# A two-layer graph kernel on one core: lookups moved from the node stage into the next stage, and logits alternated between two PSUM banks while the attention stage fills

## The reference, cut to what matters

```python
# x: 50000 nodes x 128; src, dst: 12500 edges, sorted by dst; edge_attr: 12500 x 128
def sage_mean(h, Ws, Wn, b):                      # twice, with relu between
    agg = segment_sum(h[src], dst); deg = segment_sum(1, dst)
    return h @ Ws + agg / max(deg, 1) @ Wn + b
x = layernorm(x + sage_mean(relu(sage_mean(x))))
# attention with 4 heads over the same edges, on the new x
q, k, v, e = x@Wq+bq, x@Wk+bk, x@Wv+bv, edge_attr@We+be
alpha = einsum('ehd,ehd->eh', q[dst], k[src] + e) / sqrt(128)
attn  = softmax of alpha over the edges of one dst
out   = segment_sum((v[src] + e) * attn, dst) + x@Wskip + bskip
x = layernorm(x + elu(layernorm(out)*ln_g + ln_b) @ Wlin + blin + x))
```

## Time and profile before

| what | value |
|---|---|
| time, median of 3 runs (lowest, highest) | 1630.11 us (1629.76, 1630.32) |
| the profiled execution: its own time, its span | 1631.72 us, 1629.9 us |
| PE busy | 1502.5 us, 92% |
| DVE busy | 1291.4 us, 79% |
| ACT busy | 1177.9 us, 72% |
| POOL busy | 1029.4 us, 63% |
| mean granted TensorE clock | 0.979 |

### The profile page before, as it was taken

How to read it: one execution, slowest core, us unless ns; L and a number is a source line. 1 busy time by engine, 2 the same in 40 slices (tenths; PEclk the granted TensorE clock), 3 DMA queues, 4 the chain that set the end, 5 groups by cost and what they waited for, 6 DMA issues and landing times. The chain is left out here.

```text
span 1629.9 us, 33886 instructions
## 1 busy us (share of the span) xinstructions
PE 1502.5 (92%) x7879; PEld 1046.4 (64%) x7879; DVE 1291.4 (79%) x6158; ACT 1177.9 (72%) x3174; POOL 1029.4 (63%) x1038
## 2 busy tenths in 40 slices
PE   4999999999999998899789977999999999999985
PEld 3777777777777776788556643555555555555543
DVE  5999999999999999566568864777777777777773
ACT  2999999999999998344257751677777777777773
POOL 2888888868888885577177627456555555556421
PEclk9999999999999999899989998999999999999997
DMA  2567666654444443233169863233333333333220
GB/s 79 143 162 154 158 155 163 153 152 149 149 147 149 149 148 125 61 96 95 58 195 291 283 213 93 79 85 89 88 90 86 86 89 89 89 83 89 72 51 8
DMA packets 156183, 199.52 MB, mean 122 GB/s; under 512 B 36159, under 2 KB 79342, under 8 KB 156070
## 3 DMA queue, kind: packets, MB, share of 16 engines
q1 hardware_dynamic: 127450, 160.43, 32.6%
q0 software_dynamic: 27200, 36.26, 10.2%
q10 hardware_dynamic: 1420, 1.60, 0.3%
HBM read 106.66 MB, written 100.07 MB: 127 GB/s over the span
## 5 line engine op out<-in xcount | busy, mean ns | idle before, releaser
L1379 POOL DMA_INDIRECT big<-x_tab,look x196 | 199.1, 1016 | 92.9 <-issue 36.8
L1396 POOL DMA_INDIRECT out_dram<-big,idx x98 | 99.5, 1015 | 222.6 <-PE pb L1448 146.4
L737 PEld LDWEIGHTS pb<-MG_s,big 128*128 128x128 f32 x832 | 149.5, 189 | 128.6 <-ACT big L770 112.5
L737 PE MATMUL pb<-MG_s,big 128*128 128x256 f32 x832 | 207.4, 392 | 26.6 <-ACT big L770 26.5
L746 ACT ACTIVATE big<-big 128x128 f32<-128x128 f32 x416 | 180.2, 482 | 0.0
L1668 DVE CUSTOM_DVE_ANT_0 big<-pb,big,zero 128x128 f32<-128x128 f32 x392 | 120.3, 348 | 72.7 <-PE pb L1491 72.5
L719 PE MATMUL pb<-C_s,big 128*128 128x128 f32 x832 | 161.6, 276 | 0.0
L720 PE MATMUL pb<-Ws1c_s,big 128*128 128x128 f32 x832 | 161.4, 276 | 0.0
L868 POOL TENSOR_TENSOR big<-big,cl 128x512 f32<-128x512 f32 x104 | 133.6, 1284 | 36.8 <-DVE big L842 35.8
L1108 POOL DMA_INDIRECT big<-h1e_tab,hidx x98 | 97.9, 999 | 73.0 <-POOLq L1916 33.0
L1508 PEld LDWEIGHTS pb<-Wg_s,big 128*128 128x128 f32 x784 | 103.8, 194 | 49.9 <-issue 41.9
(11 more groups left out here) (356 smaller groups left out, 4017.1 us busy)
## 6 DMA issues: line engine op xcount, KB each, us to landing
big<-in_x_dram SPq DMA_DIRECT2D x104, 256.0 KB
x_tab<-big SPq DMA_DIRECT2D x98, 256.0 KB
out_dram<-big SPq DMA_DIRECT2D x98, 256.0 KB, 2.1
c_ve<-ve_tab SPq DMA_DIRECT2D x98, 256.0 KB, 2.8
ve_tab<-c_ve SPq DMA_DIRECT2D x66, 256.0 KB
h1e_tab<-a_rows SPq DMA_DIRECT2D x25, 256.0 KB, 2.6
x_tab<-a_rows SPq DMA_DIRECT2D x25, 256.0 KB
big<-in_edge_attr_dram SPq DMA_DIRECT2D x97, 64.0 KB
```

Source lines behind the costliest of these rows:

```text
L737: t = pe.matmul(o, b_x1T[:, r * P:(r + 1) * P], MG_s[:], start=True, stop=True)
L1379: g.indirect_dma_start(out=o, out_offset=None, in_=x1_tab, in_offset=bass.IndirectOffsetOnAxis(ap=look[:, a, j:j + 1], axis=0), bounds_che ...
```

## The change

It has two parts.

**Lookups.** The slots for the small transfers in a node-stage turn are numbered anew: a turn with a source gather now has one of them, all others two. The redirect writes end in turn 53 instead of 49, the lookups begin in turn 55 (`LOOK_AT` = 101) and go on through turn 103, the last; by then 91 of the 98 are issued. The other seven, the wait for all of them and the four operations that make `hidx` move to the end of `a_pool`, in the first sampling stage. The helpers between `b_pool` and `a_pool` only change their place in the file.

**Logits.** In the fill, tiles 1, 3, 5, 7 and 9 have their logits in `VB` instead of `PB`. PE then waits for the logits of two tiles ago instead of one. Since `VB` first holds the tables of turn 0, the product of tile 1 waits for DVE's copy of them (`g_fol`), and the first values product, in turn 10, waits for the logits of tile 9. For tiles in `VB`, DVE's unused full-size output goes to `d_vex` instead of `d_junk`.

```diff
+        LOOK_AT = NT + 3
+        B_LOOKS = 2 * TILES - 4 * R - LOOK_AT
+        assert 0 < B_LOOKS < NT and TILES >= 6 * 4 * R
+        def look_up(g, e):
+            g.indirect_dma_start(out=look[:, 0, e:e + 1], out_offset=None, in_=redirect,
+                                 in_offset=bass.IndirectOffsetOnAxis(ap=idx[:, SRC, e:e + 1], axis=0),
+                                 bounds_check=N - 1, oob_is_err=False).then_inc(dma_k[e % 4], 16)
...
-                if it % 6 == 5 and it < 96:
+                brings = it % 6 == 5 and it < 6 * 4 * R
+                if brings:
                     gather_src(g, it // 6 // R, it // 6 % R)
-                for t in range(2 * it, 2 * it + 2):
+                slot = 2 * it - min(it // 6, 4 * R)
+                for t in range(slot, slot + (1 if brings else 2)):
...
-                    elif t >= TILES and t - TILES < NT:
-                        if t == TILES:
+                    elif t >= LOOK_AT:
+                        if t == LOOK_AT:
                             for k in range(4):
                                 g.wait_ge(dma_p[k], 16 * len(range(k, NT + 1, 4)))
+                        look_up(g, t - LOOK_AT)
             g.wait_ge(s_row, 16 * (TILES // 8 + (1 if spread < E else 0)))
...
+        def a_pool(g):
+            for s in range(4, NG):
+                after(g, "a_pmT", s - 4)
+                for r in range(min(R, NT - R * s)):
+                    gather_src(g, s, r)
+            for e in range(B_LOOKS, NT):
+                look_up(g, e)
             for k in range(4):
                 g.wait_ge(dma_k[k], 16 * len(range(k, NT, 4)))
             g.tensor_scalar(hf[:, 0, 0:NT], look[:, 0, 0:NT], float(N), float(FAR), ALU.is_lt,
...
+        def logit_bank(a):
+            return VB if a < LAG and a % 2 else PB
...
                     if b == 0:
                         pe.wait_ge(step("g_fol"), RUNS)
+                        after(pe, "d_al", LAG - 1)
                     values(b)
...
                     after(pe, "d_xT", a)
-                    after(pe, "d_al", a - 1)
-                    pe.matmul(PB[:], X(a, 0), Aqk_s[:], start=True, stop=False)
+                    after(pe, "d_al", a - 1 if a > LAG else a - 2)
+                    if a == 1:
+                        after(pe, "g_fol", 0)
+                    pe.matmul(logit_bank(a)[:], X(a, 0), Aqk_s[:], start=True, stop=False)
...
-                    pe.matmul(PB[:], X(a, 2), Aqe_s[:], start=False, stop=True).then_inc(step("d_pP"), 1)
+                    pe.matmul(logit_bank(a)[:], X(a, 2), Aqe_s[:], start=False, stop=True).then_inc(step("d_pP"), 1)
...
-            return v.tensor_tensor_reduce(hs(d_junk, h), hs(PB, h), d_x1d[a % XD], SCALE, zero[:, 0:1],
+            junk = d_vex if logit_bank(a) is VB else d_junk
+            return v.tensor_tensor_reduce(hs(junk, h), hs(logit_bank(a), h), d_x1d[a % XD], SCALE, zero[:, 0:1],
```

More of the change, by code:

```diff
@@ L995, in a_pool @@
                     gather_src(g, s, r)
+            for e in range(B_LOOKS, NT):
+                look_up(g, e)
+            for k in range(4):
+                g.wait_ge(dma_k[k], 16 * len(range(k, NT, 4)))
+            g.tensor_scalar(hf[:, 0, 0:NT], look[:, 0, 0:NT], float(N), float(FAR), ALU.is_lt,
+                            ALU.mult).then_inc(s_look, 1)
+            g.tensor_scalar(hf[:, 1, 0:NT], look[:, 0, 0:NT], float(-N), None, ALU.add).then_inc(s_look, 1)
+            g.wait_ge(s_look, 2)
+            g.tensor_tensor(hf[:, 1, 0:NT], hf[:, 0, 0:NT], hf[:, 1, 0:NT], ALU.add).then_inc(s_look, 1)
+            g.wait_ge(s_look, 3)
+            g.tensor_copy(hidx[:, 0:NT], hf[:, 1, 0:NT]).then_inc(s_look, 1)
+            g.wait_ge(s_look, 4)
         def a_dve(v):
```

## The result

The changed kernel took **1618.63 us** (median of four runs, 1617.88 to 1619.28) against 1630.00 for the kernel before (1629.76 to 1630.32): 11.4 us less, ratio 0.993, 95% interval 0.9913 to 0.9947. The forecast was 1627.4 with a range of 1626.1 to 1629.0, and most of its chance on a difference too small to measure. The gain came out at four times the 2.7 us of the forecast.

The account below looks back on a forecast made before the run. The prediction took DVE to bound the node stage, POOL's DRAIN its end, and PE the attention stage after a serial fill. Fill 2.3 + node-stage end 0.4 = 2.7 us off 1630.11: 1627.4, range 1626.1 to 1629.0.

Parts of the forecast that it names:

- the first term of the change: Node stage: spreading the lookups takes one small transfer out of 16 turns, changes no DVE, PE or ACT instruction; worth 0.
- DVE waiting for L878: Node stage: a sign in the changed kernel's profile that would show the prediction wrong; no size given.
- POOL's last lookup: Node stage's end: lasting 1.40 instead of 1.00 beside DVE's L837, it would end at 648.9, leaving nothing of 0.4.
- POOL's list sets nothing there as long as its addition L868 is in time: Node stage: DVE busy 595.4 of 609 us, POOL 489; L868 waits for DVE, not DVE for it.
- The node stage's end: Stage ends with POOL's DRAIN; lookups end at 648.5, DRAIN 7.4 later: gain 0.4 us, between gain 1.0 and loss 0.2.
- The operations moved: First sampling stage: seven lookups, their landing and four operations end with POOL's DRAIN at about 800, SP 809.0; cost 0.
- The fill: Attention's fill: with two logits banks PE no longer stands before each product; gain 2.3 us, bounds 0.9 and 3.2.
- Turn 1: Fill: tile 1's product waits for DVE's copy of turn 0's tables, starting at 989.09 instead of 988.17; loss 0.9.
- Tile 1's wait: Fill: PE's wait before tile 1's product, expected at about 1.8 us.
- the values': Fill: PE's wait before the first values product, for tile 9's logits, expected at 1 us or more.
- slower: the clock: Fill: PE's longer wait before tile 1's product drops its clock to the lower level; about 1636 us; chance 0.05.

## Why the prediction was wrong, step by step

- **The step that failed** is the first term of the change: "Spreading them changes no instruction of DVE, PE or ACT. It takes one small transfer out of each of the 16 turns with a source gather; with DVE nearly full in any case that is worth 0." The first sentence is true of the list and false of the durations. The term measured 9.9 to 10.1 us. DVE's 595.4 busy of 609 was read as work, but 10 of them were DVE held in one instruction. The question that was not asked: is each duration of DVE's the same in all turns? One query for L817 would have given 147, 154 and 1247 ns as its least, median and longest. The sign of error that the prediction named for this stage, DVE waiting for L878, couldn't show it: the hold leaves no wait in the trace.
- **The contention was weighed in one direction, and by half of its rule.** The prediction had the earlier trace rows: POOL is held when DVE has the way to SBUF. It costed this for POOL's last lookup alone. The trace of before shows the reverse 16 times, DVE held while POOL's addition has it. The Trainium skill (SBUF — State Buffer, SBUF: two separate sides) states it both ways: whichever of a DVE instruction "in a 2-port perf mode, or with two SBUF inputs" and a GpSimd operation starts first holds the shared pair for the whole instruction, and the other blocks; for the DVE operation with two inputs it says so only against a GpSimd operation that reads SBUF, as the addition does. The trace agrees: L817 ended with the addition, within 0.05 us, as TENSOR_SCALAR on SBUF and with two inputs from SBUF, and ran free with one input from SBUF and one from PSUM. The prediction had left the port mode out of the rule that it cited. One input in SBUF isn't enough to be held: L813, of that kind, ran beside the addition in most turns of before, and was never longer than 298 ns (270 the least, 277 the median). That it is the port mode which holds the TENSOR_SCALAR form, no run here separates.
- **"POOL's list sets nothing there as long as its addition L868 is in time"** was right as a condition, but "in time" was judged by who waits for the addition's result, not by when it ran beside DVE.
- **The node stage's end**: right. Forecast -0.4 between +0.2 and -1.0, measured -0.3; DRAIN 7.56 us after the last lookup, forecast 7.4. The operations moved cost nothing measurable: POOL's DRAIN ends at 788.7 with SP at 799.2, a cover of 10 against the forecast's 9.
- **The fill**: right in mechanism. Forecast 2.3, measured 2.0. Turn 1 lost 0.92 (4.98 to 5.90), as worked out; from there to the values product it is 25.30 instead of 28.31 us, a gain of 3.0 against a forecast 3.2. Tile 1's wait was 1.65 and the values' 1.36.
- **The rival "slower: the clock"** didn't come: PE stood 1.65 us before tile 1's product, as it assumed, and the level stayed at 1.00 from 979 to 1004. What the runs show beside it is another thing, a rise that comes a turn late. It cost 2.8 us in one execution of the logits' part, and it came with the fill of before too.

The two parts measured alone add up: 9.95 and 1.4 are 11.35, against 11.4. That it fits so closely is in part luck, as each of them is known to about 2 us and 1.5 us.

## What to carry to other kernels

Busy is not work. Where an engine is nearly full, look at the least and the longest duration of each group before calling an edit beside it worth nothing, above all of DVE's short instructions while POOL computes on SBUF. The cure need not be the slow engine's schedule: other operands for the one instruction that is held gave as much as spreading 98 transfers. And when a new wait is the price of a second buffer, see whether its other tenant can be housed elsewhere: here that shortened the stretch by 1.6 us, where the two banks with the wait had brought 2.0.

## What the runs showed of the hardware

- A 128x4 clamp on DVE takes 0.15 us, and up to 1.25 us if POOL's 128x512 addition, both operands in SBUF, began before it. The time stands in the profile as busy, with no idle time and no releaser.
- With one input from PSUM the same clamp took 0.15 us or less 104 times, whatever POOL did, and was no slower by itself (median 145 ns against 154).
- The same program took 1630, 1685 or 1695 us on different chips. Most of the difference lay in the stages with dense gathers. From SP's branch to the next the two sampling stages take 157 and 165 us in the first profile, and 174 and 205 in that of the logits' part on the chip with 1695: 57 us more, of 64 between the two spans.
